# Feed-forward layer 1 in four-byte form: two matmuls per bank in place of six on rounded high and low parts

## What is computed

```python
x = x + 0.5 * ffn(layernorm(x))
x = x + mamba(layernorm(x))
x = x + 0.5 * ffn(layernorm(x))

# ffn: gf is a small net of the mean over tokens; then three cycles of
h = gelu(out @ w1 + b1)      # 256 -> 256   layer 1
h = gelu(h @ w2 + b2)        # 256 -> 128   layer 2
h = gelu(h @ w3 + b3)        # 128 -> 64    layer 3
tf = sigmoid(h @ w4 + b4)    # 64  -> 1     layer 4
coupling = 0.1 + adaptive_range * (0.7 * gf + 0.3 * tf - 0.5) * 2
out = out + coupling * twist(out)
```

## Time and profile before

| | us |
|---|---|
| median of 3 runs | 1491.64 (1488.38 to 1492.56) |
| the profiled execution's own time | 1491.21 |
| its span, first to last instruction | 1489.4 |
| PE busy | 1140.8 (77%) |
| DVE busy | 1308.7 (88%) |
| POOL busy | 1032.9 (69%) |
| ACT busy | 776.0 (52%) |
| mean granted TensorE clock | 0.916 of full |

### The profile page before, as it was taken

How to read it: one execution, slowest core, us unless ns; L and a number is a source line. 1 busy time by engine, 2 the same in 40 slices (tenths; PEclk the granted TensorE clock), 3 DMA queues, 4 the chain that set the end, 5 groups by cost and what they waited for, 6 DMA issues and landing times. The chain is left out here.

```text
span 1489.4 us, 11591 instructions
## 1 busy us (share of the span) xinstructions
PE 1140.8 (77%) x3072; PEld 537.1 (36%) x3072; DVE 1308.7 (88%) x1793; ACT 776.0 (52%) x1348; POOL 1032.9 (69%) x470
## 2 busy tenths in 40 slices
PE   2979965469687787867868777786887677798996
PEld 2545442123242242333324324232432322454544
DVE  5897894499999989999998999999899899789777
ACT  1544434656754655764565575466557334254443
POOL 1241310698997899899799799879979999224131
PEclk8999986589998998998999899799989989799998
DMA  5000000334434433443343443344344443000001
GB/s 184 0 1 0 0 1 14 115 113 149 161 116 136 148 128 128 142 141 114 128 146 125 141 141 115 139 143 141 114 143 142 141 153 115 1 0 1 29 29 57
DMA packets 46945, 146.53 MB, mean 98 GB/s; under 512 B 4448, under 2 KB 13280, under 8 KB 46880
## 3 DMA queue, kind: packets, MB, share of 16 engines
q1 hardware_dynamic: 46384, 144.96, 29.4%
q10 hardware_dynamic: 496, 0.82, 0.2%
HBM read 141.05 MB, written 4.72 MB: 98 GB/s over the span
## 5 line engine op out<-in xcount | busy, mean ns | idle before, releaser
L969 POOL TENSOR_TENSOR m_u<-m_dx,m_brow 128x1024 f32<-128x1024 f32 x256 | 599.1, 2364 | 36.4 <-DVE m_a_bank L1065 36.3
L1229 PE MATMUL m_y_bank<-m_hc,ident 128*128 128x512 f32 x704 | 382.4, 673 | 188.5 <-DVE m_hc L1077 188.5
L848 ACT ACTIVATE m_a_bank<-m_delta,m_negA 128x512 f32<-128x512 f32 x512 | 335.1, 684 | 174.7 <-DVE m_hc L1077 136.8
L188 POOL TENSOR_TENSOR f_state_lo<-f_state,f_state_hi 128x512 fp32r<-128x512 f32 (+1 forms) x64 | 122.4, 1925 | 251.8 <-DVE f_state_hi L202 251.8
L1229 PEld LDWEIGHTS m_y_bank<-m_hc,ident 128*128 128x128 f32 x704 | 135.3, 207 | 419.1 <-DVE m_hc L1077 293.8
L1065 DVE TENSOR_TENSOR_SCAN m_a_bank<-m_a_bank,m_carry,m_u 128x512 f32<-128x512 f32 x176 | 216.7, 1281 | 12.4 <-POOL m_u L969 12.4
L1077 DVE TENSOR_TENSOR m_hc<-m_a_bank,m_crow 128x512 f32<-128x512 f32 x352 | 224.5, 684 | 0.0
L981 POOL TENSOR_TENSOR m_hc_pool<-m_hid,m_crow 128x1024 f32<-128x1024 f32 x80 | 189.1, 2363 | 49.0 <-DVE m_hid L1065 48.9
L1065 DVE TENSOR_TENSOR_SCAN m_a_bank<-m_a_bank,m_u 128x512 f32<-128x512 f32 x176 | 206.0, 1220 | 10.6 <-POOL m_u L969 9.7
L1229 PE MATMUL m_y_bank<-m_hc_pool,ident 128*128 128x512 f32 x320 | 151.2, 595 | 0.3 <-POOL m_hc_pool L981 0.3
L1192 PE MATMUL m_w_bank<-m_xn,w 128*128 128x512 f32 x240 | 116.9, 610 | 5.5 <-DVE m_x L1124 5.5
(11 more groups left out here) (132 smaller groups left out, 1606.1 us busy)
## 6 DMA issues: line engine op xcount, KB each, us to landing
m_brow<-bc_rows SPq DMA_DIRECT2D x128, 512.0 KB, 4.8
m_crow<-bc_rows SPq DMA_DIRECT2D x128, 512.0 KB, 4.0
x_tok<-x_in SPq DMA_DIRECT2D x4, 1024.0 KB, 8.7
out<-x_tok SPq DMA_DIRECT2D x3, 1024.0 KB, 4.4
w<-w_in SPq DMA_DIRECT2D x1, 1024.0 KB, 12.3
out<-x_tok SPq DMA_DIRECT2D x2, 512.0 KB, 3.0
w<-w_in SPq DMA_DIRECT2D x1, 750.0 KB, 10.3
w<-w_in ACTq DMA_DIRECT2D x1, 512.0 KB, 6.0
```

The source lines that it names most:

```text
L188: nc.gpsimd.tensor_tensor(state_lo[:, :, cs], state[:, :, cs], state_hi[:, :, cs].bitcast(F32), ALU.subtract).then_inc(split, 1)
L848: nc.scalar.activation(a_bank[K % 2][:, j, :], delta[:, i % 2, c, :], ACT.Exp, scale=negA[:, c, n:n + 1]).then_inc(S["a"], 1)
L969: nc.gpsimd.tensor_tensor(u[:, K % U_RING, :, :], dx[:, i % 2, 2 * q:2 * q + 2, :], brow[:, K // 2 % ROW_RING, K % 2, :].unsqueeze(1).to_b ...
L1229: op = nc.tensor.matmul(y_bank[:, j, :], ident[:, :], source[:, before % ring, j, :], start=False, stop=K % PASS == POOL_N[-1])
```

## The change

Layer 1 multiplies `state` and the weights as they are, in float32: two matmuls per bank, as layer 2 does. With that go the tensors `state_hi`, `state_lo`, `w1_hi`, `w1_lo` and their semaphores, DVE's roundings, the weight split, and all of POOL's work in `ffn`. PE waits for the writer of the state itself (ACT's copy of the "in" bank, or DVE's `update`). DVE, which had waited for the weights in `split_w1`, does so ahead of the small constants.

```diff
-        state_hi = sb("state_hi", [P, KD, BATCH * SEQ], F32R)
-        state_lo = sb("state_lo", [P, KD, BATCH * SEQ], F32R)
-        w1_hi = sb("w1_hi", [P, KD, DIM], F32R)
-        w1_lo = sb("w1_lo", [P, KD, DIM], F32R)
...
-        @block.gpsimd
-        def _(pool):
-            for n, job in enumerate(SPLITS):
-                cs = split_columns(job)
-                pool.wait_ge(rounded, n + 1)
-                nc.gpsimd.tensor_tensor(state_lo[:, :, cs], state[:, :, cs], state_hi[:, :, cs].bitcast(F32),
-                                        ALU.subtract).then_inc(split, 1)
...
             for t in range(4):
                 normalise(0, t)
-            if load_sem is not None:
-                split_w1()
-            for t in range(4):
-                round_state("in", 0, t)
             moments_of((1,))
...
             normalise(1, 3)
-            for t in range(4):
-                round_state("in", 1, t)
+            if load_sem is not None:
+                dve.wait_ge(load_sem["weights"], 48)
...
                     for h in range(HALVES):
                         update(s - 1, h)
-                        if cycle(s - 1) < CYCLES - 1:
-                            round_state("update", s - 1, h)
-                    for kind, b, t in [u for k in range(5) for u in due(s - 1, k)]:
-                        if kind == "in" and b > 1:
-                            round_state("in", b, t)
...
-                job = ("in", b, 2 * h + 1) if cycle(s) == 0 else ("update", s - 2, h)
-                pe.wait_ge(split, SPLITS.index(job) + 1)
+                if cycle(s) == 0:
+                    wait_read(pe, ("in", b, 2 * h + 1))
+                else:
+                    pe.wait_ge(updated, updates(s - 2, h))
                 cs = slice(b * SEQ + h * BANK, b * SEQ + (h + 1) * BANK)
-                passes = [(k, wt, st) for k in range(KD)
-                          for wt, st in ((w1_lo, state_hi), (w1_hi, state_lo), (w1_hi, state_hi))]
-                for n, (k, wt, st) in enumerate(passes):
-                    last = nc.tensor.matmul(bank[h * 2 + m][:, :], wt[:, k, m * P:(m + 1) * P], st[:, k, cs],
-                                            start=n == 0, stop=n == len(passes) - 1)
+                for k in range(KD):
+                    last = nc.tensor.matmul(bank[h * 2 + m][:, :], w(w256, W256, "w1", k)[:, m * P:(m + 1) * P],
+                                            state[:, k, cs], start=k == 0, stop=k == KD - 1)
```

More of the change, by code:

```diff
@@ L145, in ffn @@
         updated, stored = sem("updated"), sem("stored")
-        w1_split, rounded, split = sem("w1_split"), sem("rounded"), sem("split")
         block = ctx.enter_context(nc.Block())
@@ L193, in _ @@
             chain = Chain(dve, base_ready)
[L195 to L202, removed]
             def moments_of(batches):
@@ L292, in measure @@
                     nc.vector.bn_aggr(moments[:, t, :], stats[:, t, :])
-            def split_w1():
-                if load_sem is not None:
[L296 to L301, removed]
             moments_of((0,))
-            if load_sem is None:
-                split_w1()
             invert((0,))
@@ L461, in _ @@
                 pe.wait_ge(load_sem["weights"], 48)
-            pe.wait_ge(w1_split, 2)
             for s in range(STEPS):
```

## The result

| | before | after |
|---|---|---|
| median, us | 1491.44 (4 runs, 1488.38 to 1492.56) | 1470.22 (3 runs, 1468.09 to 1471.64) |
| ratio | | 0.9853, 95% interval 0.9834 to 0.9872 |
| profiled execution, us | 1491.2 | 1468.8 |

The kernel is 1.5% faster; one disturbed execution of 2913.66 us is left out.

A forecast was written before the change was run, and what follows sets the result against it. It took DVE to set the pace in steps 2 to 5, a loop through all engines in 9 to 11. Gains of 5.0 us (`f1`) and 4.8 (`f2`), together 9.8, took 1491.2 to 1481.4, median about 1481.5; range 1474 to 1490.

The forecast's parts named there:

- step 0: Start of each feed-forward block: earlier transposes less the price of three layer-1 banks, +2.9 us in `f1` and in `f2`.
- step 1: PE's wait for ACT's table loads hides two of four banks; the other two cost 0.7 us in each block.
- one [bank] at low clock (0.95): Step 0 of `f1`: one of three layer-1 banks runs at low clock and costs 0.95 us more.
- upper branch: Step 0 of `f2`: gain about 4.1 us if the clock stays high, against 1.5 if it stays low.
- The first bank no longer matters: Step 0 of `f1`: the first layer-1 bank ends ahead of PE's wait for transposes, so its price was not counted.
- clearly faster: Rival: full clock from the first transposes on and in step 1 of both blocks, 5.7 us more, 1476; chance 0.10.
- The price of 0.34 per bank: Layer 1 on PE: a float32 bank takes 1.72 us where the F32R bank took 1.38.
- Back come 4.8 us: Steps 6 to 11 of `f1`: PE's waits for `state_lo` (3.5 us) and a late `add_back` (1.3) go.
- DVE as the bound of steps 2 to 5: Steps 2 to 5: DVE sets the pace through split work; without it, +6.2 us in `f1`, +6.3 in `f2`.
- nearer 0.43: Within-0.3% rival, first way: layer 1's price per bank is nearer 0.43 us, giving 1489; chance 0.18 for both ways.
- half of the idle time stays: Within-0.3% rival, second way: half of PE's 18 us idle in steps 2 to 5 stays, 1490; chance 0.18 for both.
- 1.91 in every bank: Slower rival: layer-1 banks pay the isolated layer-2 price of 1.91 us, +0.53 for 90 banks, 1499; chance 0.06.

The follow-up runs named there:

- e6_before_fill: The kernel before, with ten matmuls into an idle bank, results unused, put in PE's two gaps of step 0 of each block: 1485.24 us, ratio 0.9964.
- e3_f32r_no_pool: The kernel before without POOL's subtractions; layer 1 still six F32R matmuls, all on the state's high part, low part left out: 1447.70 us, ratio 0.9712.
- e1_split_unread: The kernel after with the whole split put back (DVE's roundings, POOL's subtractions) and read by nobody: 1501.06 us, ratio 1.0069.
- e2: The kernel after with DVE's roundings and the weight split put back, read by nobody, and no POOL work: 1475.15 us, ratio 0.9896.
- e4: The kernel after with one unread POOL subtraction of the state from itself per written piece, no roundings on DVE: 1475.39 us, ratio 0.9895.
- e7: The kernel after with the four unused split tensors allocated again and never touched: 1470.43 us, ratio 0.9867.
- e10: The kernel of e9_dve_split with layer 1 in float32 also in steps 4 and 5, and in 10 and 11 of `f1`: 1458.95 us, ratio 0.9795.
- e5_one_group: The kernel after with layer 1 on the first group of 128 features alone, half of its sum left out: 1406.64 us, ratio 0.9429.
- e9_dve_split: The kernel after with layer 1 of cycles 2 and 3 in six split passes, rounding and subtraction both on DVE: 1463.22 us, ratio 0.9813.

## Why the prediction was right in direction and wrong in size

In profiled time 22.9 us of span were gained where 9.8 were forecast. By stage, for `f1` and `f2`, cut at layer 1 as in the forecast:

| | forecast | measured | miss, both blocks |
|---|---|---|---|
| step 0 | +2.9, +2.9 | +5.5, +4.1 | 3.7 |
| step 1 | -0.7, -0.7 | +1.0, +0.9 | 3.3 |
| steps 2 to 5 | +6.2, +6.3 | +7.0, +7.1 | 1.6 |
| steps 6 to 11 | -3.4, -3.7 | -1.9, -2.2 | 3.0 |
| scan block | 0 | +1.4 | 1.4 |

- **The step that failed is the clock in steps 0 and 1** (7.0 of the 13 us missed). The prediction kept "one [bank] at low clock (0.95)" in `f1`'s step 0, took the middle between low and full clock in `f2`'s, and booked step 1 at the price of two banks alone. The transposes came when it said: 4.6 us earlier in `f1` (33.39 to 28.76; forecast 4.55) and 3.1 in `f2`. What it missed is that from there to the end of step 1 the clock would not fall. e6_before_fill measures what the clock had cost there at 7.3 us. In `f2` its own upper branch, "about 4.1 if the clock, PE having no gap, stays high", is what was measured, 4.1; it booked 2.9. "The first bank no longer matters" was right for the order of the waits and wrong for the clock: ahead of that bank PE had waited 3.57 us for POOL in `f1` and 2.22 in `f2`, the clock fell there, and the change takes both waits away. The rival "clearly faster" named the mechanism and its place, but sized it at 5.7 and gave it 0.10. Its reason against, the waits that stay, was the wrong reading: they stay, but shorter (1.70 and 1.14 us).
- **Step 1's two banks** were right: 15.61 against 14.96 in e6_before_fill, 0.65 for two.
- **The price of 0.34 per bank** was right where PE never waits (0.33 and 0.34 over whole steps). Over the stages less of it is paid, 16 banks at 4.74 us and 24 at 7.62 (82.59 less 74.97, cut at layer 1), because in e3_f32r_no_pool some of the time saved goes into waits of 0.4 and 0.8 us. That is 2 x (16 x 0.34 - 4.74) + 2 x (24 x 0.34 - 7.62) = 2.5 us of the miss.
- **"Back come 4.8 us"** in steps 6 to 11, and 4.5 in `f2`, were mis-sized: the waits were worth 5.7 and 5.5. Why the profile's idle time falls short was not tried; a likely reason is that a matmul's record ends later than its follower could start (layer-1 records of 0.39 at a pitch of 0.23), so that each wait reads too short.
- **A slip without weight:** the bank at low clock, 3.44 less 2.41, is 1.03 us and not 0.95.
- **DVE as the bound of steps 2 to 5**: right for steps 4 and 5, as e1_split_unread shows, and not for 2 and 3, where PE had waited for 0.9 us in all before the change. The sum holds all the same, since it took PE's idle time over the four steps together. "Because of work that is there only for the split" was right too, but it took both halves of that work together.
- **The other rivals** (nearer 0.43, half of the idle time stays, 1.91 in every bank) did not occur. Steps 2 to 5 came to 55.68 for the forecast 56.5, steps 6 to 11 to 82.6 for 84, PE above 98%: the signs it named all stood.

What stays open: the exact condition for the clock's fall. With a gap of 1.1 us in step 1 it never fell (after, e1, e2, e4 and e7 to e10, both blocks). With 1.8 it fell in the kernel before in both blocks and in `f1` of e3_f32r_no_pool, and not in e3's `f2` or e6_before_fill. In step 0 it stayed up behind 2.32 us (e3, `f1`) and 3.19 us (e1, `f2`), and in step 4 of the kernel before 3.31 us had both outcomes. The gap alone doesn't decide it. So the end of the clock's falls is shown, and that shorter waits brought it about is argued from these rows; no run shortened a wait by itself.

## What to carry to other kernels

Price a shorter wait on TensorE twice: the wait itself, and the half clock behind it, which here was worth more than everything else that the prediction got wrong. More PE work can be the faster choice when the cheaper form needs two other engines to prepare it: test each preparer alone, since here, behind step 0, either one was nearly free and both together cost 9 us in each block. And compare a helper engine with the bound at the operation that is waited for, not by its mean per step.

## What the runs showed of the hardware

- A float32 matmul of 128x512 takes 0.86 us at full clock, two records of 0.43 (3.44 us per plain step for four of them, e5_one_group); three `F32R` ones take 0.69 (1.37 per six, e3_f32r_no_pool).
- A gap of 2.85 us in PE's work was followed by a bank of layer 2 in 3.78 us (1.98 after), and one of 2.22 by a clock of 0.75 over 6 us (e9_dve_split); one of 1.70 by full clock. The same gap of 3.31 us in the same kernel was followed by a clock of 0.50 over 4 us in one block and of 1.00 in the other.
- Beside GpSimd's subtraction, DVE's normalising of a tile rose from 408 to 753 ns in the mean, and a two-input product from 693 to 1391 (e4_pool_unread, 20 to 110); a rounding of 128x512 rose from 421 to 1136 (e1_split_unread).
- DVE's own subtraction of 128x1024 (two inputs in SBUF) takes 1.23 us where GpSimd takes 2.58.
